# One common set of five PSUM banks for scores and row maxima, and a max pass planned a twentieth of a group earlier

## What is computed

```python
xn = layernorm(x)
# attention, 16 heads of 16: q and k are rotated (rope), causal
scores = einsum('bhqd,bhkd->bhqk', q, k) / sqrt(16)
probs = softmax(where(causal, scores, -1e9))
attn = einsum('bhqk,bhkd->bhqd', probs, v) ... @ Wo.T
# feed-forward with 9 paths, of which each token takes one
xm = mix over three neighbouring tokens of xn
h = einsum('bsd,pdm->bspm', xm, W1) + b1
paths = einsum('bspm,pmd->bspd', h, W2) + b2
idx = argmax(tanh(xm @ Wo1 + bo1) @ Wo2 + bo2)
ffn = layernorm(xn + paths[idx]) * gamma + beta
out = x + attn + ffn
```

## Time and profile before

| | |
|---|---|
| median of 3 runs | 783.06 us (782.4 to 784.2) |
| the profiled execution | 784.09 us, of which its span is 782.4 us |
| PE busy | 739.9 us, 95% |
| DVE busy | 641.7 us, 82% |
| ACT busy | 448.9 us, 57% |
| POOL busy | 288.3 us, 37% |
| mean granted TensorE clock | 0.974 |

### The profile page before, as it was taken

One profiled execution on the slowest core, in us unless ns is written; L12 is line 12 of the kernel. 1 busy time (PEld: TensorE's weight loads), 2 busy tenths in 40 slices (PEclk: granted clock), 3 DMA queues, 4 the chain that ended last, 5 costly groups with the idle time before them and its releaser, 6 DMA issues.

```text
span 782.4 us, 12591 instructions
## 1 busy us (share of the span) xinstructions
PE 739.9 (95%) x4416; PEld 372.3 (48%) x4416; DVE 641.7 (82%) x1894; ACT 448.9 (57%) x780; POOL 288.3 (37%) x459
## 2 busy tenths in 40 slices
PE   4869999999999999999999999999999999999996
PEld 2432344354565544345465544445465554354544
DVE  5989999889798789888988789897988669878622
ACT  2262645765655654775656655666657555754672
POOL 2001123990615112893514213695334203130623
PEclk9965999999999999999999999999999999999999
DMA  7259050224613434112651615111560705100103
GB/s 242 97 164 191 8 114 2 72 81 113 105 15 59 105 91 77 53 60 83 118 72 28 136 56 112 33 69 53 122 109 2 136 28 112 33 2 2 28 1 81
DMA packets 40577, 59.98 MB, mean 77 GB/s; under 512 B 4813, under 2 KB 36830, under 8 KB 37634
## 3 DMA queue, kind: packets, MB, share of 16 engines
q1 hardware_dynamic: 36002, 54.39, 29.4%
q0 software_dynamic: 4224, 4.19, 4.1%
q10 hardware_dynamic: 288, 0.59, 0.2%
HBM read 42.04 MB, written 16.85 MB: 75 GB/s over the span
## 4 chain that ended last, share of the span: by engine, by line
PE 71%; POOL 10%; DVE 8%; ACT 6%; DMA 2%; issue 1%; SPq 1%; POOLq 0%; ACTq 0%; DVEq 0%
PE bank L1557 14%; PE bank L1538 14%; PE bank L1519 14%; PE bank L1500 7%; PE bank L1510 6%; PE bank L1462 3%; POOL prob L1014 3%; PE bank L1585 3%; PE bank L1473 3%; ACT prob L1132 3%; POOL raw L993 2%; POOL turned L991 2%; PE bank L1480 2%; PE bank L1567 2%; POOL turned L999 1%
## 5 line engine op out<-in xcount | busy, mean ns | idle before, releaser
L1132 ACT ACTIVATE prob<-bank 128x512 f32<-128x512 f32 x576 | 324.6, 597 | 194.4 <-PE bank L1538 191.3
L1350 DVE CUSTOM_DVE_ANT_0 bank<-bank,causal_sb 128x384 f32<-128x384 f32 (+3 forms) x512 | 240.3, 513 | 34.3 <-PE bank L1519 33.5
L1519 PE MATMUL bank<-k_st,q_st 96*128 96x512 bf16 (+3 forms) x768 | 236.1, 339 | 8.4 <-DMA q_st<-scratch 4.0
L1014 POOL TENSOR_SCALAR_AFFINE_SELECT prob<-prob 128x256 f32<-128x256 f32 (+1 forms) x320 | 125.9, 427 | 294.0 <-ACT prob L1132 291.1
L1538 PE MATMUL bank<-q_st,k_st 98*128 98x512 bf16 (+3 forms) x768 | 212.4, 331 | 7.9 <-ACT prob L1132 5.8
L1353 DVE TENSOR_REDUCE piecemax<-bank 128x1 f32<-128x512 f32 x256 | 164.0, 683 | 18.6 <-PE bank L1519 18.2
L1557 PE MATMUL bank<-prob,v_sb 128*17 128x512 f32 (+3 forms) x1536 | 143.9, 495 | 0.8 <-POOL prob L1014 0.8
L1519 PEld LDWEIGHTS bank<-k_st,q_st 96*128 96x128 bf16 x768 | 72.4, 98 | 130.8 <-DVE piecemax L1350 49.4
L1538 PEld LDWEIGHTS bank<-q_st,k_st 98*128 98x128 bf16 x768 | 70.0, 98 | 113.7 <-ACT prob L1132 56.7
L1510 PE MATMUL bank<-w_sb,mid 128*128 128x256 f32 (+1 forms) x320 | 83.7, 383 | 0.0
L1462 PE MATMUL bank<-xnT,wqk_sb 128*128 128x512 f32 x128 | 68.3, 639 | 4.6 <-ACT xnT L1079 3.7
(11 more groups left out here) (82 smaller groups left out, 698.7 us busy)
## 6 DMA issues: line engine op xcount, KB each, us to landing
scratch<-parts SPq DMA_DIRECT2D x16, 768.0 KB, 3.8
q_st<-scratch SPq DMA_DIRECT2D x90, 128.0 KB, 6.8
k_st<-scratch SPq DMA_DIRECT2D x15, 384.0 KB, 4.6
z<-in_x SPq DMA_DIRECT2D x8, 512.0 KB, 4.5
mask<-chosen SPq DMA_DIRECT2D x16, 256.0 KB
z<-in_x POOLq DMA_DIRECT2D x8, 512.0 KB, 6.7
out<-z SPq DMA_DIRECT2D x8, 512.0 KB, 4.7
k_st<-scratch SPq DMA_DIRECT2D x15, 256.0 KB, 5.4
```

Of the source, the lines that this page charges most:

```text
L1014: nc.gpsimd.affine_select(out=d, in_=d, compare_op=ALU.is_ge, fill=0.0, base=0, pattern=pattern, channel_multiplier=-1).then_inc(masked, 1)
L1132: nc.scalar.activation(prob[:, place_of(G, i), :], ps[:, :], ACT.Exp, scale=float(DK) ** -0.5).then_inc(act_took, 1)
L1350: nc.vector.tensor_tensor_reduce(ps, ps, causal_sb[:, HALF - w:HALF], 1.0, NEG, ALU.add, ALU.max, to).then_inc(dve_took, 1)
L1519: nc.tensor.matmul(begin(("max", G, u))[:, 0:w], q_st[0:PARTS, G % STACKS, h, t * P:(t + 1) * P], k_st[0:PARTS, G % STACKS, h, k0:k0 + w], ...
```

## The change

Scores units chose between banks 1 and 2, max units between 3, 4 and 5. Now both choose among 1 to 5, still the one given out longest ago, so that the five go round in the order of use of both kinds together. For what is ordered ahead of time 0, other units keep 1, 2, 6 and 7, and max units get 1 to 5. The max pass of the groups from 2 on is spread over G - 1.0 to G - 0.03 where it was G - 0.95 to G + 0.03; cut, shift and place of the second half hang on its end, those of the first half on its 16th unit, and move with it. Groups 0 and 1 keep their times. The order is written anew from these inputs.

```diff
@@ -220,7 +220,7 @@
                 add(at + 4.5 / NS, "oT", G, half)
 
         units = range(len(FIRST_UNITS), NM) if G == 0 else range(NM)
-        a, e = (0, 0.22) if G == 0 else (G - 0.75, G + 0.02) if G == 1 else (G - 0.95, G + 0.03)
+        a, e = (0, 0.22) if G == 0 else (G - 0.75, G + 0.02) if G == 1 else (G - 1.0, G - 0.03)
         for u in units:
             at = a + (e - a) * (u - units[0]) / len(units)
             add(at, "max", G, u)
@@ -321,7 +321,7 @@
 def bank_choice(at, what):
     if at < 0 and what not in ("max", "shift"):
         return (1, 2, 6, 7)
-    return {"S": (1, 2), "max": (3, 4, 5)}.get(what, (6, 7))
+    return (1, 2, 3, 4, 5) if what in ("S", "max") else (6, 7)
```

## The result

| | median us (range, runs) | against before, 95% interval |
|---|---|---|
| before | 783.63 (782.4 to 785.66, 4) | |
| after | 793.03 (790.54 to 796.9, 4) | 1.0122 [1.0072, 1.0171] |

The change makes the kernel 1.2% slower: +9.4 us (5.6 to 13.4 by the interval) where -4 was forecast, 14 us above the forecast time and 4 us beyond the end of the wider range.

The account below looks back on a forecast made before the run. PE's own work was taken to set the pace, with ACT and DVE unbroken in bursts. Terms -4 +1 -1 +0 = -4 us took 784.09 to 780 (779 against the median); range 775 to 781.4, for 8 in 10 770 to 789.

Parts of the forecast that it names:

- What bounds the kernel: Whole span: PE's own work mostly sets the pace; in bursts PE waits for unbroken ACT and DVE.
- a price of 0.13 us for each short wait of a weight load: Burst at 678 to 684 us: ten waits cost PE 1.34 us, 0.13 each; 293 waits at most 38 us.
- Banks, net -4 us: Steady part, 75 to 735 us: scores gain 7 us, max units lose 3; bounds nothing back to 16 us.
- The shared queue, +1 us: Scores may wait for banks behind DVE's 39 own jobs between maxima; 1 us lost, bounds 0 and 12.
- The end, -1 us: After 754 us: five banks let PE run ahead and cut ACT's gaps; 1 us gained, bounds 0 and 2.3.
- The lead, 0 (-1 to +2): Max pass of groups 2 to 15 planned 2.2 to 2.6 us earlier; fills stay hidden, no cost.
- The clock: Rival: new waits drop PE to 1.2 GHz for 20 us, 793; chance 0.05, shared with a crowded start.
- slower, by the shared queue: Rival: scores units wait for DVE's own jobs between maxima; 786 to 790 us, chance 0.25.
- No change: Rival: ACT and DVE are unbroken in bursts and five banks stay five; 783 us, chance 0.18.

Follow-up runs that it names:

- e13: Kernel before with the common set of five banks, and POOL waiting for DVE's normalization before its third rope product of each batch row; 782.63 us.
- e16: Kernel before with only POOL's added wait for DVE's normalization before its third rope product of each batch row; 782.73 us.
- e3: Kernel before with its written order kept on every engine, but scores and max units taking banks from the common set of five; 793.07 us.
- e6: Kernel before with the common set of five banks for what is due up to group 15, split banks behind it, old lead; 792.53 us.
- e9: Changed kernel with the fills of groups 5, 9 and 13 written behind the shift DMAs of groups 3, 7 and 11; 787.41 us.
- e18: Changed kernel with shift DMAs ahead of the fills and the second-half cuts, shifts and places of groups 1, 5 and 9 moved up; 791.51 us.
- e14: Changed kernel with shift DMAs ahead of the fills and POOL waiting for DVE's normalization before its third rope product; 787.5 us.
- e1: Kernel before with the common set of five banks only, the max pass keeping its old due times; 789.53 us.

## Why the prediction was wrong

**What bounds the kernel** was read rightly in one half. The statement that in the bursts "PE waits for two engines that have no more to give" is what the runs bear out. The other half, a price of 0.13 us for each short wait of a weight load, doesn't hold as a price of time: e13 has 256 bank waits of 96.8 us where e16, with the banks of before, has 286 of 110.5, and the times are 782.63 and 782.73. At 0.13 us each the 30 waits would have been 4 us; they gave 0.1 by the medians and at most some 1.5.

**Banks, net -4 us.** The waits of scores for exponentials fell as said (125 to 49 and 70). The term's value is near 0: 0.0 and -0.1 us between the medians of the two pairs with the collision away (some 1.5 us by the ratios of one pair). It was mis-sized; the lower bound, nothing back, was nearly right, and the unbroken engines in the burst of the earlier trace rows had pointed there.

**The shared queue, +1 us.** With the old order it costs 9 us (e3), with the order that the planner writes for it nothing that can be seen. The planner's foresight was the right argument. But it knows only its table of costs: it wrote a new order at the start in which DVE's normalization falls under six of POOL's rope products and takes 7.9 us (131.66 to 139.5) where the table has 2.2. This is the +5.2 us of banks only (e13: 789.53 becomes 782.63 with nothing left out), and no term or rival of the prediction had it.

**The end, -1 us.** ACT's gaps went as forecast, and gave nothing (e6, and e13 beside e16): PE waits for POOL instead, 2.26 us for 0.77. The prediction named POOL as the next engine and still took a gain. In the changed kernel's profile the granted clock of that stretch is 0.95, so a part of it ran at 1.2 instead of 2.4 GHz, behind PE's waits between 769 and 778 us; the last projection took 5.38 us, where e13, with the same waits and a clock of 1.00, has 3.69. That is 1.7 us of this one profile.

**The lead, 0 (-1 to +2).** This is the step that failed most. "8.2 us of slack become about 6, so SP's nine DMAs of a fill stay hidden" was true of the fill, and no max unit waited for one. What was missed is who is queued behind it: the shift DMAs are due earlier with the lead, and SP issues them right behind the fill. In the changed kernel that is 5.6 us (e9). The lead alone costs 5.9 us with few waits for shift DMAs (2.4 us), half of it 13, a thousandth nothing: so the cost does not follow the slack; that it depends on which pieces meet in an order written anew is what is left, argued and not shown. What the 3.3 us are that e9 leaves over the kernel before, and what makes the half lead so dear, stays open; for the former the late cut (e18) and the collision with the rope (e14) were tried and are not it, for the latter the late cut is about 2 us of 13.

**The clock** is a candidate for part of it, seen in the profiles and tested by no run. The prediction read 1.00 in three stretches of the kernel before; in a fourth the clock was lower, and with the lead alone it was so in five windows of 10 us in which PE was all but full. First the lead only, then the kernel before, then PE's timeline of the lead only:

```profile
280.00:290.00 10.00, 9.86 (x46) 3.34 (x45) 9.23 (x33) 4.78 (x8) 1.57 (x5) 0.66 0.16 52
460.00:470.00 10.00, 9.69 (x49) 4.15 (x48) 8.25 (x25) 5.54 (x10) 0.58 (x2) 0.74 0.32 107
650.00:660.00 10.00, 10.00 (x55) 3.42 (x54) 8.55 (x21) 6.26 (x12) 2.92 (x9) 0.87 0.21 53
```
```profile
280.00:290.00 10.00, 9.98 (x58) 3.67 (x57) 7.63 (x26) 4.98 (x10) 1.99 (x6) 0.83 0.09 28
460.00:470.00 10.00, 9.98 (x79) 4.55 (x67) 8.85 (x31) 4.22 (x9) 1.34 (x5) 1.00 0.18 57
```
```profile
277.80 1.95 PE L1487 MATMUL bank<-wo_sb,hidden_e 64*128 64x9 f32 x16
...
282.84 0.63 PE L1538 MATMUL bank<-q_st,k_st 98*128 98x512 bf16 x1
283.27 0.63 PE L1519 MATMUL bank<-k_st,q_st 96*128 96x512 bf16 x1
283.69 0.63 PE L1538 MATMUL bank<-q_st,k_st 98*128 98x512 bf16 x1
```

At a clock of 0.50 its matmuls of 512 columns start 0.43 us apart, where the earlier trace rows have 0.22. The clock was at 0.50 from 280.5, 464.8 and 649.1 us on, for 6.8, 6.8 and 3.4 us, and each time it fell within 1 us behind the 16 matmuls of nine columns of L1487. The kernel before and the changed kernel have this run in the same places of their orders, once per batch row; of the last three the kernel before shows a fall behind the first (281.5 us), the changed kernel behind the third (649.0). Why behind some and not others is open. Half of these 17 us, 8.5 us, is what the lower clock can have cost there, against 1.7 us in the kernel before (3.4 us at 0.50). The difference of 6.8 us would be the whole loss of the lead alone, but it is an upper estimate: DVE was nearly full in some of these windows too, and other waits of PE changed as well. The mean clock of all runs points the same way: 0.967 with the lead alone, 0.969 with half of it, 0.970 in the changed kernel and in e9, 0.976 before; the changed kernel's four runs took 790.54 us at 0.972 and 796.9 at 0.966.

**The rivals.** The sign was that of "slower, by the shared queue", but its mechanism, scores behind maxima (39 places in the changed kernel), is a small part at most: e13 has 42 such places of 16.3 us and costs nothing. Both causes that were found (the shift DMAs behind a fill, small DVE jobs under POOL's) stood in no rival. "No change" is what the banks by themselves are worth, within some 1.5 us. "The clock" gave 793 for one fall of 20 us. That the measured time is the same is luck: the falls in the profiles are shorter, and 5.6 us have another cause.

**In sum**, of the +9.4 us: 5.6 by the order at SP (shown, e9), the rest of 3 to 4 us not settled; it comes with the lead, as the banks alone cost nothing once their collision is away, and a lower granted clock may be part of it. The common set's own loss of 5 us (e1) is another collision, which the changed kernel's order hardly has; the parts don't add up, 5.2 and 5.9 alone and 9.4 together, because each new order meets other neighbours. Of all versions that leave no work out the kernel before with POOL's wait (782.73) and the common set with it (782.63) are the best, the second 0.3% faster than before in its set of runs; the intervals of the two overlap.

## What to carry to other kernels

When a change makes a planner write the order anew, the change's own effect may be smaller than that of the neighbours that it brings together. Hold the old order fixed and change the part, hold the new order and take the part back, and run a placebo; three runs say which of the two one is looking at. In a list of short waits on a full engine, ask which other engine would have to be faster for the wait to be worth something. Read the granted clock of each variant in short windows as well: a mean of 1.00 over 50 us says nothing of the windows elsewhere. A step that is "hidden" on a DMA queue isn't costed until the one behind it is: 1.0 us at SP behind a fill became 2.1 us on PE.

## What the hardware showed that was not expected

- DVE instructions on SBUF operands run at a POOL job's pace while POOL multiplies in SBUF: 0.16 us became 1.15 to 1.29 us, and four normalizations of 0.35 us became 5.05 us; one DVE instruction went through per POOL instruction of 1.27 us. Maxima that read PSUM were not stretched: 0.28 to 0.33 us (L1350, 128 columns) in e13 at 134 us, under a rope product.
- Two DMAs of 4 KB issued right behind a fill let PE wait until 9 us after their issue ended (213.6 to 222.86 us in the changed kernel), while a load of 512 KB that POOL had issued at 208.99 was under way too; issued ahead of a fill, at 212.89, they kept no scores waiting at 222.06.
- In stretches in which PE's rows leave hardly a gap the granted clock fell to 0.50 for 3 to 7 us (280.5 to 287.3 us with the lead alone, 649.0 to 652.4 in the changed kernel), behind 16 matmuls of nine columns; matmuls of 512 columns then started 0.43 us apart instead of 0.22.
